# A selective scan whose products by C are shared between VectorE and GpSimd: ten and six of each sixteen instead of eight and eight

## What is computed

```python
def step(h, inp):
    u_t, d_t, b_t, c_t = inp
    dA = jnp.exp(d_t[:, :, None] * A)
    h = dA * h + (d_t * u_t)[:, :, None] * b_t[:, None, :]
    y = jnp.einsum('bdn,bn->bd', h, c_t)
    return (h, y)
...
delta = jax.nn.softplus(dt @ p['Wdt'] + p['bdt'])
y = _selective_scan(xc, delta, A, Bm, Cm, p['Dp'])
y = y * jax.nn.silu(z)
return x + y @ p['Wblk']
```

## Time and profile before

| what | value |
|---|---|
| median of 3 runs | 2284.54 us (2284.45 to 2295.04) |
| the profiled execution | 2288.18 us |
| its span, first to last instruction | 2286.4 us |
| TensorE (matmul) busy | 1921.3 us, 84% |
| VectorE busy | 1951.5 us, 85% |
| ScalarE busy | 1687.4 us, 74% |
| GpSimd busy | 1508.2 us, 66% |
| mean granted clock of TensorE | 0.923 of full speed |

### The profile page before, as it was taken

How to read it: one execution, slowest core, us unless ns; L and a number is a source line. 1 busy time by engine, 2 the same in 40 slices (tenths; PEclk the granted TensorE clock), 3 DMA queues, 4 the chain that set the end, 5 groups by cost and what they waited for, 6 DMA issues and landing times.

```text
span 2286.4 us, 35098 instructions
## 1 busy us (share of the span) xinstructions
PE 1921.3 (84%) x10784; PEld 1205.6 (53%) x10784; DVE 1951.5 (85%) x1824; ACT 1687.4 (74%) x3050; POOL 1508.2 (66%) x1365
## 2 busy tenths in 40 slices
PE   4688888888888888888888788888887689999998
PEld 1444444444444444444444444444444368998998
DVE  3799898998999998998999999998999976776776
ACT  3888888888888888888888888888888423333333
POOL 2688888888888888888888888888888700000000
PEclk8899998999999999999999999998999889999999
DMA  7323222222222323232323223222322200000000
GB/s 233 80 66 74 66 73 58 73 58 73 58 73 58 74 59 75 60 76 59 75 61 77 75 66 76 65 76 60 76 62 66 92 1 10 10 11 10 9 6 10
DMA packets 81482, 139.49 MB, mean 61 GB/s; under 512 B 21264, under 2 KB 39312, under 8 KB 76816
## 3 DMA queue, kind: packets, MB, share of 16 engines
q1 hardware_dynamic: 75024, 120.36, 20.5%
q10 hardware_dynamic: 6400, 18.42, 3.3%
HBM read 63.85 MB, written 7.74 MB: 31 GB/s over the span
## 4 chain that ended last, share of the span: by engine, by line
PE 34%; ACT 23%; POOL 17%; issue 11%; DVE 7%; ACTq 1%; POOLq 0%; DVEq 0%
PE y_ps L1215 10%; ACT decay L545 9%; POOL scan L466 8%; PE dbu_ps L1191 8%; POOL scan L460 8%; PE dbu_ps L1015 6%; PE pre_ps L1028 5%; ACT scan L623 5%; DVE scan L799 5%; PE pre_ps L1038 2%; POOL scan L457 2%; ACT sp_e L582 1%; ACT delta L583 1%; PE y_ps L1000 1%; ACT sp_l L592 1%
## 5 line engine op out<-in xcount | busy, mean ns | idle before, releaser
L799 DVE TENSOR_TENSOR_SCAN scan<-decay,dbu_ps 128x1024 f32<-128x1024 f32 x512 | 1157.3, 2276 | 151.4 <-PE dbu_ps L1015 147.1
L466 POOL TENSOR_TENSOR scan<-scan,c_rep 128x1024 f32<-128x1024 f32 x256 | 722.8, 2823 | 263.3 <-DVE scan L799 190.0
L1015 PE MATMUL dbu_ps<-ident,scan 128*128 128x128 f32 x4096 | 605.3, 296 | 287.3 <-DVE scan L799 181.9
L1015 PEld LDWEIGHTS dbu_ps<-ident,scan 128*128 128x128 f32 x4096 | 505.3, 152 | 619.7 <-DVE scan L799 303.8
L545 ACT ACTIVATE decay<-d_rep,a_cur 128x510 f32<-128x510 f32 x1024 | 670.7, 710 | 138.3 <-DMA d_rep<-delta 82.5
L460 POOL TENSOR_SCALAR scan<-du_t,b_t 128x256 f32<-128x256 f32 x896 | 591.5, 677 | 0.0
L623 ACT ACTIVATE scan<-du_t,b_t 128x256 f32<-128x256 f32 x1024 | 442.5, 494 | 1.2
L808 DVE TENSOR_TENSOR scan<-scan,c_rep 128x1024 f32<-128x1024 f32 x256 | 328.0, 1281 | 0.0
L1000 PE MATMUL y_ps<-scan,sel 128*32 128x512 f32 x2048 | 300.5, 661 | 5.7 <-POOL scan L466 5.7
L737 ACT ACTIVATE decay<-dbu_ps 128x512 f32<-128x512 f32 x256 | 148.6, 598 | 209.8 <-PE dbu_ps L1191 198.7
L1028 PE MATMUL pre_ps<-xn,w_pre 128*128 128x512 f32 x512 | 274.5, 663 | 5.7 <-DVE w_pre L788 4.9
(11 more groups left out here) (105 smaller groups left out, 1737.7 us busy)
## 6 DMA issues: line engine op xcount, KB each, us to landing
d_rep<-delta SPq DMA_DIRECT2D x1024, 64.0 KB, 2.0
c_rep<-c_rows SPq DMA_DIRECT2D x32, 1024.0 KB
w_pre<-prepared_weights ACTq DMA_DIRECT2D x15, 866.0 KB, 10.4
prepared_weights<-scan SPq DMA_DIRECT2D x3, 1122.0 KB, 23.9
scan<-in_conv_w SPq DMA_DIRECT2D x4, 512.0 KB, 4.6
w_out<-prepared_weights SPq DMA_DIRECT2D x16, 128.0 KB, 9.8
sp_e<-in_x_rows SPq DMA_DIRECT2D x8, 256.0 KB, 3.3
d_rep<-in_w ACTq DMA_DIRECT2D x2, 1024.0 KB, 7.5
```

The costliest lines, as they stand in the source:

```text
L466: nc.gpsimd.tensor_tensor(ring[slot % RING], ring[slot % RING], c_rep[par][:, slot // PRS, :].unsqueeze(1).broadcast_to([128, 2, TG]), ALU ...
L799: nc.vector.tensor_tensor_scan(ring[slot % RING].rearrange("p u t -> p (u t)"), decay[slot % DEC].rearrange("p u a t -> p (u a t)"), dbu_p ...
L1015: last = nc.tensor.transpose(dbu_ps[slot % 2][:, u, 128 * j:128 * j + 128], dbu_t[m % 2][:, j, b, :, :].rearrange("p q c -> p (q c)"), ide ...
```

## The change

Two products of each step move from GpSimd to VectorE: x7 and x15. The lists of who makes which product become constants, and the counts that other engines wait for follow them.

```diff
+C_DVE = [c for c in range(M * PRS) if c % 2 == 0 or c % 8 == 7]
+C_POOL = [c for c in range(M * PRS) if c not in C_DVE]
...
-                    if slot == 0 and has(s, -1):
-                        times_c(s - 1, i if par else i - 1, nxt, SLOTS - 1)
-                    elif slot % 2 == 0 and slot and has(s, 0):
+                    if slot - 1 in C_POOL and has(s, 0):
                         times_c(s, i, par, slot - 1)
...
                     if has(s, 0):
                         scan(s, slot)
-                        if slot % 2:
+                        if slot - 1 in C_DVE:
                             times_c(s, i, par, slot - 1)
+                        if slot == SLOTS - 1:
+                            times_c(s, i, par, slot)
...
             def quad(s, m, k):
-                pe.wait_ge(hc_dve, SLOTS // 2 * s + 2 * m + k + 1)
-                pe.wait_ge(hc_pool, SLOTS // 2 * s + 2 * m + k + 1)
+                end = PRS * m + 2 * k + 2
+                pe.wait_ge(hc_dve, len(C_DVE) * s + sum(c < end for c in C_DVE))
+                pe.wait_ge(hc_pool, len(C_POOL) * s + sum(c < end for c in C_POOL))
```

More of the change, by code:

```diff
@@ L389, in window @@
                     sp.wait_ge(skip_done, STEPS)
-                    sp.wait_ge(hc_dve, SLOTS // 2 * (STEPS - 1))
-                    sp.wait_ge(hc_pool, SLOTS // 2 * (STEPS - 1))
+                    sp.wait_ge(hc_dve, len(C_DVE) * (STEPS - 1))
+                    sp.wait_ge(hc_pool, len(C_POOL) * (STEPS - 1))
                     for e in range(EXPERTS):
@@ L570, in copy_dbc @@
                 act.wait_ge(dbc_ready, s + 1)
-                wait(act, hc_dve, SLOTS // 2 * (s - 1))
-                wait(act, hc_pool, SLOTS // 2 * (s - 1))
+                wait(act, hc_dve, len(C_DVE) * (s - 1))
+                wait(act, hc_pool, len(C_POOL) * (s - 1))
                 act.dma_start(c_dram[par, :, :], dbc[RANK + NS:NBC, :]).then_inc(c_stored, 16)
```

## The result

The changed kernel takes 2323.45 us (median of 4 runs, 2321.45 to 2324.06), the kernel before 2284.49 us on the same chip. The ratio is 1.0164, 95% interval 1.0126 to 1.0203: slower, with the interval clear of 1; whether by as much as 2% it leaves open. The forecast was 2283.2 us, no change; the rival in which x15 keeps the ports stood at 2318 us. The profiled execution has a span of 2321.6 us against 2286.4, 35.2 us more.

A forecast was written before the change was run, and what follows sets the result against it. The end of round 0 on GpSimd was taken to set each step's start. 30 steps by minus 0.02 us and minus 0.7 for the last two gave minus 1.3, 2283.2 us against the median; own range 2279 to 2291, 8 in 10 2270 to 2297.

The forecast's parts named there:

- the rival in which x15 keeps the ports: At GpSimd's last instruction of round 0: held 1.11 us more in each of 31 steps, 34 us; chance 0.11.
- The loop: Step start on TensorE, ScalarE's softplus parts, VectorE's softplus and one scan, GpSimd from x9 to round 0's end, TensorE again.
- x7: Before VectorE's softplus: plus 0.30 us, less 0.32 from shorter softplus instructions; minus 0.02 us per step.
- x15 on VectorE: Behind x14, before the next first scan: covered by 2.59 us of waiting, GpSimd gets in between; 0 us per step.
- The row from the prologue: Four like VectorE instructions, each about 0.6 us; GpSimd's line 438 waited 0.40 us, read as getting in between two.
- The two last steps: Steps 30 and 31: plus 0.8 us for x7 in step 30, with step 31's terms a sum of minus 0.7 us.
- that part of the sum (1.1 + 1.1 - 4.1 + 0.4): Step 31: x7 1.1, x15 1.1, VectorE's cast freed of GpSimd's x15 minus 4.1, x14 held by experts' additions 0.4 us.
- The clock rival: TensorE's clock falls at other moments, changing the mix of short and long steps: 2271 us (0.13) or 2295 us (0.05).

The follow-up runs named there:

- x7 alone: Against the changed kernel, x15 stays on GpSimd and only product x7 moves to VectorE; 2279.28 us, ratio 0.999 to the kernel before.
- the gap: Changed kernel, but x15 waits for a semaphore that x14 counts up at its end; 2275.67 us, ratio 0.9975 to the kernel before.
- x15 late: Changed kernel, but x15 alone stands behind the first scan of the next step; 2287.84 us, ratio 1.0008 to the kernel before.
- the scalar from SBUF: Changed kernel, but x15 is a scalar_tensor_tensor that also multiplies by 1.0 read from SBUF; 2274.71 us against 2282.21 before, one run.
- the kernels with x14 late: x14 behind the next step's first scan: in the kernel before, ratio 0.9806; in the changed kernel with x15 there too, 0.9877; with x7 moved, 0.9818.

## Why the prediction was wrong

**The loop was right.** Every experiment that changed the time to the end of round 0 moved the kernel with it, and those that left it at 1.89 us (x7 alone, the gap, x15 late, the scalar from SBUF) left the kernel within half a percent of before. No reading of the busy shares gives that: VectorE is at 86% in the kernel that is slower.

**x7 was right.** It was put at minus 0.02 us per step; scan 8 to scan 9 changed by 0.01 us in the step shown, by 0.4 us in the sum of 30 steps (209.9 to 209.5), and the kernel by nothing that can be measured. Lines 834 and 838 fell from 1.38 to 1.225 us, as their first step had shown.

**x15 on VectorE is the step that failed**: "So a waiting GpSimd instruction gets in between two VectorE instructions, and the second of these waits." The bounds there were 0 and 1.11 us per step, and 0 was taken. What the runs showed in its place is that GpSimd's instruction waits over x14 and x15: 1.06 (2.49 - 1.43), and 1.15 for a whole step. The place and the price of the rival were right; its chance of 0.11 was too low. The row from the prologue was real, but of another kind of instruction: those VectorE instructions take a scalar from SBUF, and the two products don't. They have no gap between them either (12.70 + 0.67 against 13.28 in the earlier trace rows), and neither have x14 and x15 (1022.49 + 1.26 against 1023.68), so the gap isn't what tells these two pairs apart. The softplus rows were no better a guide, since each of its instructions waits for a semaphore of the one before. In this case GpSimd wasn't let in across the pair of products, and was where a wait or a scalar's read from SBUF came with the second.

The Trainium skill, page "SBUF — State Buffer", section "SBUF: two separate sides", says that the ports are held for the whole instruction, that the other engine blocks fully, and that the hardware doesn't drain its queues to share them. The runs agree: GpSimd's instruction takes 1.43 us beside one product. That the one who starts first keeps them, as the prediction gives it from the same section, isn't what was measured for two products in a row: GpSimd's instruction is noted at 1022.66 and x15 at 1023.68, and x15 went first.

**The two last steps** were put at minus 0.7 us. From the last `delta` to the end of the span, step 31 and the experts, it is 533.1 us before and 532.1 after, minus 1.0, where that part of the sum (1.1 + 1.1 - 4.1 + 0.4) was minus 1.5. But the same stretch is 528.6 to 534.2 us in the other kernels of the study, so the total says little. The two largest terms can be seen by themselves: the cast's stretch fell by 4.17 us (5.68 to 1.51), and from scan 8 to scan 9 of the last step it is 3.31 us instead of 2.20, x7's full price.

**The clock** isn't the cause of the loss. The mean granted clock is 0.923 in both profiled executions, and the steps that begin with transposes of the slow kind are 21 before and 22 after. It has a small part: the 5.5 us between scan 0 and scan 8 go with the lower clock there, and it may be in the medians, which are 39 us apart where the two spans are 35.2. The clock rival didn't decide the change, but in the kernels with x14 late the faster transposes gave about half as much as the hold.

## What to carry to other kernels

When an instruction goes to an engine with room, ask what else it occupies. Here 1.11 us of VectorE's idle time were free, but GpSimd could not work beside the product that filled them, and so the engine that the edit relieved became late. Put a VectorE instruction with two inputs from SBUF where GpSimd's work is not on the path, or let it wait for the one before it; the existing x14 was the same fault, and moving it past the next scan gained 1.9%, 30 us by the hold and the rest with TensorE's clock. A row that shows how two engines take turns holds for that form of instruction, with its waits and operands; look for a row of the same form before calling a rival unlikely.

## What the runs showed of the hardware

GpSimd waits for a VectorE product, whose two inputs are in SBUF: its 0.46 us instruction takes 1.43 beside one, and 2.49 beside two that follow without a gap. The second product then shows no stretch (1.21 us). A semaphore wait between the two (2.67 us for the pair) or a scalar operand read from SBUF in the second (1.49 us for it, against 1.21 with a constant) lets the waiting GpSimd instruction in, 1.89 and 1.90 us for the two instructions of round 0. Scans, whose second input is in PSUM, don't hold GpSimd: x13 lies beside two of them (1019.87 to 1022.23 against 1018.12 to 1022.57) and takes 2.36 us, where x9 beside a product takes 3.26.

TensorE's eight transposes take 1.96 us at a granted clock of 0.50 and 1.09 at 1.00.
